# A mixture-of-experts stage: the weights of each of 32 experts are loaded once into a ring of eight, and TensorE finds a tile's weights by a register

## The chip, the cores and the metric

The kernel runs on one core of one Trainium2 chip. The metric is the device time of one execution in microseconds (us); lower is better. The core has a matrix engine (TensorE, called PE in the profile, with PEld for its weight loads), three engines that work on vectors (VectorE or DVE, ScalarE or ACT, GpSimd or POOL) and SyncE (SP), which here issues the transfers from device memory (HBM) into the on-chip memory. Each engine runs its own list of instructions; the lists meet in semaphores. Names such as PEldq and SPq are the sequencers of these engines, which run register work and bare waits.

## The reference

The program is a small two-layer decoder on 4 x 256 tokens of width 256. Layer 0 has cross-attention over 1601 context rows and then a mixture of experts, layer 1 has windowed attention and a feed-forward with weights rounded to 8-bit floats. The part that matters here is the mixture of experts of layer 0:

```
scores  = sigmoid(x @ gate_w)                       # 1024 tokens x 32 experts
selected = top 6 of the experts in the allowed groups
for each expert e and its tokens xs:                # 6144 rows in all
    d = (silu(xs @ w_gate[e]) * (xs @ w_up[e])) @ w_down[e]   # 256 -> 176 -> 256
out = sum over a token's 6 rows of weight * d  +  a shared expert of twice the width
```

## The kernel before, in words

The stage is the function `experts`. It first works out, on VectorE and TensorE, how many tokens each expert has. An expert's rows are cut into tiles of 128 rows, and the tiles of all experts stand one after the other in 80 slots (`NSLOT`; slots beyond the last tile are worked on too, with an empty token). The table `expert_of` (1 x 80, int32) says which expert a slot belongs to.

The loop runs over 96 jobs. The first 16 (`SHARED`) are the halves of the shared expert for the eight blocks of 128 tokens; their weights lie on chip. Jobs 16 to 95 are the 80 slots. For slot i the work is:

- POOL gathers the tile's rows (`gather`, L1445), eleven slots ahead, and scatters its results (`scatter`, L1450).
- PE turns the rows (`turn_rows`, L1494), multiplies them with gate and up weights (`gate_up`, L1506), turns the hidden tile (`turn_hidden`, L1513) and multiplies it with the down weights (`down`, L1523 and L1524).
- ACT applies silu (L1548) and copies the turned rows and the results (L1553, L1558).
- DVE multiplies silu with up (`hidden`, L1630) and copies the turned hidden tile out to `moe_hT` (`hidden_turned`, L1635).

All orders are written out by hand. In step j PE does `gate_up(j)`, `turn_rows` for two jobs later, `down(j - 2)` and `turn_hidden(j - 1)`. So in PE's list the down projection of one job is followed by the turn of the next job and the up projection of the one after that. In step j DVE does `hidden(j)`, `hidden_turned(j - 1)` and, in every second step from job 28 to job 90 (32 times), one part of `quantize` (L1662 to L1672): ten dependent instructions that round the weights of the last layer.

The weights lie in a ring of eight places, `wa` (gate, up and most of down, 480 KB) and `wb` (the rest of down, 48 KB). SP fills one place for each slot (`fetch`): it reads the slot's expert number into a register, and issues two transfers from the address that it gives. Slot i uses place i % 8, so PE's addresses are constants. A place is filled anew when the slot eight before has finished (`y_done`). PE waits, ahead of `gate_up`, for the count of the place's own semaphore (`load`), and ahead of `down` for the copy of the hidden tile (`ht_sb`) and for the release of its output (`added`, `y_sb`). Most waits stand on an instruction; where there are several, the others become bare wait instructions (EVENT_SEMAPHORE) on the sequencer, which the profile puts on L92 (the helper `wait`) or L1502.

Of the kernel before, what the change touches and what calls it, by code (L numbers as in the profile page):

```python
# [7 lines left out]
I32 = mybir.dt.int32  # L8
U32 = mybir.dt.uint32
F16 = mybir.dt.float16  # L10
ALU = mybir.AluOpType
# [4 lines left out]
P = 128  # L16
B, S, D = 4, 256, 256
# [3 lines left out]
DC = D // P  # L21
# [1133 lines left out]
E_ALL, TOPK, GRP, TOP_GRP = 32, 6, 4, 2  # L1155
M = 176
EXPERTS = E_ALL + 2
GU = 2 * M
REST = M - P
WA = DC * GU + D  # L1160
NSLOT = 80
# [5 lines left out]
SHARED = 2 * TT  # L1167
JOBS = SHARED + NSLOT
WRING, XRING, YRING = 8, 12, 4
CONST = {}  # L1170
for _name, _width in (("tri", P), ("before", E_ALL), ("upto", E_ALL), ("lane", P), ("slot", NSLOT), ("tokm", TT), ("spare", NSLOT), ("turn", TOPK), ("zero", D)):
    CONST[_name] = slice(sum(c.stop - c.start for c in CONST.values()), sum(c.stop - c.start for c in CONST.values()) + _width)
NCONST = CONST["zero"].stop
NCAST = CONST["upto"].stop
SPAN = 512
# [177 lines left out]
def experts(nc, t, x, wabs, wvo, wq):  # L1353

    with Scope(nc, "moe") as sc:
# [13 lines left out]
        tiles_of = sc.sb("tiles_of", [E_ALL, P], BF16)  # L1369
        raw = sc.sb("raw", [E_ALL, P])  # L1370
        last_tile, begun = sc.sb("last_tile", [E_ALL, 1]), sc.sb("begun", [E_ALL, NSLOT], BF16)
        expert_of = sc.sb("expert_of", [1, NSLOT], I32)
        base = sc.sb("base", [P, E_ALL])
        v = sc.sb("v", [P, TT, E_ALL])
        first8 = sc.sb("first8", [P, TT, 8])
# [9 lines left out]
        shared_a, shared_b = sc.sb("shared_a", [P, 2, WA]), sc.sb("shared_b", [REST, 2, D])  # L1385
        names = ["w8_in", "const_in", "shared_in", "ident_in", "zero_out", "ones_set", "pad_set", "cast_done",
                 "rank_done", "count_done", "tiles_ready", "base_done", "begun_ready", "expert_done", "expert_ready", "index",
                 "hot", "table_part", "table_ready", "rows_ready",
                 "xt_done", "xt_sb", "up_done", "silu_done", "h_done", "ht_done", "ht_sb", "y_done", "y_sb", "added", "quant", "share_step"]
        s = {n: sc.sem(n) for n in names}  # L1390
        load, stored, gathered, back = ([sc.sem(f"{n}{i}") for i in range(r)] for n, r in (("load", WRING), ("stored", YRING), ("gathered", XRING), ("back", 2)))

# [2 lines left out]
            (shared_a[:, e, :], t["wa_l"][E_ALL + e], s["shared_in"]) for e in range(2)] + [  # L1395
            (shared_b[:, e, :], t["wb_l"][E_ALL + e], s["shared_in"]) for e in range(2)] + [(w8[:, :], t["f8_l"], s["w8_in"])])
        wa, wb = sc.sb("wa", [P, WRING, WA]), sc.sb("wb", [REST, WRING, D])
        xg = sc.sb("xg", [P, XRING, D])
        xT = sc.sb("xT", [P, 3, DC, P])
        silu, h = sc.sb("silu", [P, 2, M]), sc.sb("h", [P, 2, 2 * P])  # L1400
# [3 lines left out]
        up_ps = [sc.ps(f"up{i}", [P, 512]) for i in range(2)]  # L1404
# [3 lines left out]
        count_ps, base_ps, last_ps = xt_ps[1][0:E_ALL, 0:P], xt_ps[1][:, P:P + E_ALL], xt_ps[1][0:E_ALL, P + E_ALL:P + 2 * E_ALL]  # L1408
        expert_ps, token_ps = xt_ps[1][0:E_ALL, 192:192 + NSLOT], xt_ps[1][:, 272:272 + 2 * NSLOT]

        with nc.Block() as block:
            @block.sync
            def _(sp):
                sp.wait_ge(s["const_in"], 16)
                sp.dma_start(t["xrow_s"][EMPTY:EMPTY + 1, :], const[0:1, CONST["zero"]]).then_inc(s["zero_out"], 16)
                sp.wait_ge(s["expert_ready"], 1)

                def fetch(i, u):
                    e = sp.value_load(expert_of[0:1, i:i + 1] if isinstance(i, int) else expert_of[0:1, bass.ds(i, 1)], min_val=0, max_val=E_ALL - 1)
                    sp.dma_start(wa[:, u, :], t["wa_l"][bass.ds(e, 1)].rearrange("e p n -> p (e n)")).then_inc(load[u], 16)  # L1420
                    sp.dma_start(wb[:, u, :], t["wb_l"][bass.ds(e, 1)].rearrange("e p n -> p (e n)")).then_inc(load[u], 16)

                for u in range(WRING):
                    fetch(u, u)
                with sp.Fori(1, NSLOT // WRING) as r:
                    for u in range(WRING):
                        sp.wait_ge(s["y_done"], r * WRING + (SHARED + u - WRING + 1))
                        fetch(r * WRING + u, u)
                for u in range(YRING):
                    sp.wait_ge(stored[u], 16 * (NSLOT // YRING))  # L1430
                for n in range(TT):
                    wait(sp, s["added"], SHARED + TOPK * (n - 1) if n > 1 else 0)
                    rows = t["y_s"][0:UNUSED, :].rearrange("(k t) d -> t k d", k=TOPK)
                    sp.dma_start(y6[:, n % 2, :, :], rows[n * P:(n + 1) * P]).then_inc(back[n % 2], 16)
# [27 lines left out]
            def _(pe):  # L1462
                def rank_and_count():
# [5 lines left out]
                    for n in range(TT):  # L1469
                        for m in range(n):  # L1470
                            nc.tensor.matmul(rank_ps[:, n, :], ones[:, :], selb[:, m, :], start=m == 0, stop=False)
                        last = nc.tensor.matmul(rank_ps[:, n, :], cast[:, CONST["tri"]], selb[:, n, :], start=n == 0, stop=True)
                    last.then_inc(s["rank_done"], 1)
# [16 lines left out]
                def turn_rows(i):  # L1490
# [3 lines left out]
                        last = nc.tensor.transpose(xt_ps[i % 2][:, c * P:(c + 1) * P], xg[:, i % XRING, c * P:(c + 1) * P], ident[:, :])  # L1494
                    last.then_inc(s["xt_done"], 1)

                def gate_up(j):
                    i = j - SHARED
                    wait(pe, s["h_done"], j - 1)
                    if i >= 0:  # L1500
                        pe.wait_ge(s["xt_sb"], i + 1)
                        pe.wait_ge(load[i % WRING], 32 * (i // WRING + 1))  # L1502
                    for c in range(DC):
                        rows = xT[:, i % 3, c, :] if i >= 0 else h32[:, c, j // 2 * P:(j // 2 + 1) * P]
                        w = wa[:, i % WRING, :] if i >= 0 else shared_a[:, j % 2, :]
                        last = nc.tensor.matmul(up_ps[j % 2][:, 0:GU], rows, w[:, c * GU:(c + 1) * GU], start=c == 0, stop=c == DC - 1)  # L1506
                    last.then_inc(s["up_done"], 1)

                def turn_hidden(j):
# [6 lines left out]
                def down(j):  # L1516
                    i = j - SHARED
                    pe.wait_ge(s["ht_sb"], j + 1)
                    wait(pe, s["added"], min(j - 1, SHARED))
                    wait(pe, s["y_sb"], i - 1)  # L1520
                    wd = wa[:, i % WRING, DC * GU:WA] if i >= 0 else shared_a[:, j % 2, DC * GU:WA]
                    we = wb[:, i % WRING, :] if i >= 0 else shared_b[:, j % 2, :]
                    nc.tensor.matmul(y_ps[j % 2][:, 0:D], hT[:, j % 3, 0, :], wd, start=True, stop=False)  # L1523
                    nc.tensor.matmul(y_ps[j % 2][:, 0:D], hT[0:REST, j % 3, 1, :], we, start=False, stop=True).then_inc(s["y_done"], 1)  # L1524

# [43 lines left out]
            def _(dve):  # L1569
                V = nc.vector  # L1570
                steps = [0]

                def link(ins):
                    steps[0] += 1
                    ins.then_inc(s["index"], 1)
                    dve.wait_ge(s["index"], steps[0])
# [4 lines left out]
                def tiles_and_slots():  # L1581
                    dve.wait_ge(s["const_in"], 16)
                    V.tensor_copy(cast[:, :], const[:, 0:NCAST]).then_inc(s["cast_done"], 1)
                    dve.wait_ge(s["count_done"], 1)
                    link(V.tensor_scalar(raw[:, :], count_ps, 1.0 / P, DOWN_HALF, ALU.mult, ALU.add))
                    V.tensor_scalar(tiles_of[:, :], raw[:, :], ROUND, -ROUND, ALU.add, ALU.add).then_inc(s["tiles_ready"], 1)
                    dve.wait_ge(s["base_done"], 1)
                    link(V.tensor_scalar(base[:, :], base_ps, -1.0, FAR, ALU.mult, ALU.add))
                    link(V.tensor_copy(last_tile[:, :], last_ps[:, 0:1]))
                    V.tensor_scalar(begun[:, :], const[0:E_ALL, CONST["slot"]], last_tile[:, 0:1], None, ALU.is_ge).then_inc(s["begun_ready"], 1)  # L1590
                    dve.wait_ge(s["rank_done"], 1)
                    link(V.scalar_tensor_tensor(v[:, :, :], rank_ps, -1.0, wide(base[:, :].unsqueeze(1)), ALU.mult, ALU.add))
                    link(V.tensor_tensor(v[:, :, :], v[:, :, :], sel[:, :, :], ALU.mult))
                    for n in range(TT):
                        last = V.max(first8[:, n, :], v[:, n, :])
                    link(last)
                    link(V.tensor_scalar(slot[:, :, :], first8[:, :, 0:TOPK], -1.0, FAR, ALU.mult, ALU.add))
                    link(V.tensor_scalar(tile_no[:, :, :], slot[:, :, :], 1.0 / P, -DOWN_HALF, ALU.mult, ALU.add))
                    link(V.tensor_scalar(tile_no[:, :, :], tile_no[:, :, :], ROUND, -ROUND, ALU.add, ALU.add))
                    link(V.scalar_tensor_tensor(lane_no[:, :, :], tile_no[:, :, :], -float(P), slot[:, :, :], ALU.mult, ALU.add))  # L1600
                    dve.wait_ge(s["expert_done"], 1)
                    V.tensor_scalar(expert_of[:, :], expert_ps[0:1, :], float(E_ALL - 1), None, ALU.min).then_inc(s["expert_ready"], 1)
# [618 lines left out]
```

## Time and profile before

| what | value |
|---|---|
| device time, median of 3 runs (lowest, highest) | 1879.2 us (1877.37, 1879.74) |
| the profiled execution: its own time | 1879.65 us |
| the profiled execution: span from first to last instruction | 1877.9 us |
| PE busy over the span | 1699.2 us (90%) |
| DVE busy over the span | 1413.8 us (75%) |
| HBM read, written | 111.73 MB, 25.86 MB |
| first expert tile's up projection, last one's | from 1344.0, 1577.2 us |

The times of one execution are read from the hardware profiler. Matmuls are pipelined and their ends are modelled, so a busy PE is not PE at its peak. Times in the views are microseconds from the start of the span. An entry such as "0.26 <-DVE moe_hT L1635" says how long the engine was idle before an instruction and what released it; "issue" is idle time in which it waited for nothing that the profile shows.

### The profile page before, as it was taken

The numbers are of one execution on the slowest core, as the hardware profiler recorded it, in microseconds if no ns is written. First come the engines' busy times: TensorE is split into PE (matmuls) and PEld (weight loads), VectorE is DVE, ScalarE is ACT, GpSimd is POOL, SyncE is SP. The second block draws the span as 40 slices with busy tenths as digits, with TensorE's granted clock in tenths as the row PEclk, the third lists the DMA queues.
The fourth block names the chain that finished last, engine by engine and source line by source line (L and its number), as shares of the span: only waits on it lengthen the run. The fifth ranks groups of instructions, "written<-read, shape, count | busy, mean of one in ns | idle before, by whom it ended". The sixth has DMA issues, their size and how long they took to land. (4 is left out here: it accounts for less than half of the span.)

```text
span 1877.9 us, 41481 instructions
## 1 busy us (share of the span) xinstructions
PE 1699.2 (90%) x14533; PEld 1305.7 (70%) x14679; DVE 1413.8 (75%) x3752; ACT 1096.8 (58%) x2774; POOL 1099.4 (59%) x1718
## 2 busy tenths in 40 slices
PE   4799999999999999999999999978999997289988
PEld 3677777878787788777877887756555553139974
DVE  7898887888977878878778788757566664675646
ACT  6577777767777667767676676642133332173534
POOL 5678695686776957967768568300366663181210
PEclk8899999999999999999999999997999998596998
DMA  3210110011011000200010000445298994500100
GB/s 125 74 51 30 60 58 30 19 36 47 18 38 36 18 19 18 63 27 18 20 36 18 24 1 24 148 142 206 72 280 269 273 269 153 152 11 24 46 9 23
DMA packets 74649, 140.24 MB, mean 75 GB/s; under 512 B 10921, under 2 KB 44818, under 8 KB 74194
## 3 DMA queue, kind: packets, MB, share of 16 engines
q1 hardware_dynamic: 63634, 105.37, 18.4%
q0 software_dynamic: 9984, 30.42, 4.7%
q8 instruction: 120, 1.97, 0.4%
q10 hardware_dynamic: 832, 1.84, 0.3%
q14 instruction: 79, 0.65, 0.1%
HBM read 111.73 MB, written 25.86 MB: 73 GB/s over the span
## 5 line engine op out<-in xcount | busy, mean ns | idle before, releaser
L920 DVE TENSOR_TENSOR att_pT<-att_pT 128x512 bf16<-128x512 f32 (+1 forms) x512 | 321.0, 650 | 165.9 <-ACT att_pT L729 162.9
L565 PE MATMUL att_out<-att_V,att_pT 128*128 128x128 bf16 x5760 | 386.8, 219 | 13.9 <-DVE att_pT L920 12.1
L565 PEld LDWEIGHTS att_out<-att_V,att_pT 128*128 128x128 bf16 x5760 | 349.0, 98 | 40.7 <-DVE att_pT L920 24.3
L729 ACT ACTIVATE att_pT<-att_pT 128x512 bf16<-128x512 f32 (+1 forms) x512 | 278.0, 572 | 128.8 <-PE att_pT L551 128.8
L735 ACT ACTIVATE att_prob<-att_scores,att_negmax 128x512 f32<-128x512 f32 (+1 forms) x512 | 330.3, 655 | 17.3 <-DVE att_negmax L909 16.9
L542 PE MATMUL att_scores<-att_K,att_Q 128*128 128x512 bf16 (+1 forms) x1408 | 298.3, 359 | 7.1 <-DVE att_Q L881 0.4
L907 DVE TENSOR_REDUCE att_mx<-att_scores 128x1 f32<-128x512 f32 (+1 forms) x512 | 291.3, 630 | 0.7 <-PE att_scores L542 0.6
L551 PE MATMUL att_pT<-att_ident,att_prob 128*128 128x128 f32 x1920 | 274.2, 274 | 0.0
L542 PEld LDWEIGHTS att_scores<-att_K,att_Q 128*128 128x128 bf16 x1536 | 150.5, 98 | 143.9 <-issue 1.7
L551 PEld LDWEIGHTS att_pT<-att_ident,att_prob 128*128 128x128 f32 x1920 | 208.6, 141 | 0.8
L465 PE MATMUL att_aux<-att_wkv,att_kvT 128*128 128x256 bf16 x1350 | 167.2, 273 | 17.8 <-DVE att_aT L881 15.3
L653 POOL TENSOR_TENSOR att_scaled<-att_kvraw,att_kw 128x256 f32<-128x256 f32 (+1 forms) x123 | 89.9, 731 | 135.7 <-ACT att_kvraw L697 135.7
L465 PEld LDWEIGHTS att_aux<-att_wkv,att_kvT 128*128 128x128 bf16 x1350 | 128.0, 98 | 35.6 <-DVE att_aT L881 18.8
L655 POOL TENSOR_TENSOR att_cosd<-att_scaled,att_tab 128x256 f32<-128x256 f32 (+2 forms) x153 | 127.1, 831 | 12.0
L1450 POOL DMA_INDIRECT y_s<-moe_ysb,moe_result_row x80 | 79.3, 991 | 77.3 <-ACT moe_ysb L1558 77.3
L667 POOL TENSOR_TENSOR att_rs<-att_rs,att_nhalf 128x2 f32<-128x2 f32 (+2 forms) x153 | 122.6, 801 | 0.0
L1548 ACT ACTIVATE moe_silu<-moe_up 128x176 f32<-128x176 f32 x96 | 30.5, 318 | 142.9 <-PE moe_up L1506 142.9
L1445 POOL DMA_INDIRECT moe_xg<-xrow_s,moe_token_row x80 | 77.6, 970 | 60.3 <-DVE moe_token_row L1617 35.9
L735 ACT ACTIVATION_READ_ACCUMULATOR att_prob<-att_scores,att_negmax 128x1 f32 x512 | 109.5, 214 | 0.0
L1506 PE MATMUL moe_up<-moe_wa,moe_xT 128*128 128x352 f32 x320 | 107.9, 460 | 0.0
L697 ACT ACTIVATE att_kvraw<-att_aux 128x512 f32<-128x512 f32 x120 | 68.7, 572 | 40.4 <-PE att_aux L465 40.1
L662 POOL TENSOR_TENSOR att_rs<-att_kss,att_eps 128x2 f32<-128x2 f32 (+1 forms) x123 | 30.6, 249 | 96.9 <-DVE att_kp L891 96.9
(342 smaller groups left out, 3230.2 us busy)
## 6 DMA issues: line engine op xcount, KB each, us to landing
moe_wa<-in_wa_l SPq DMA_DIRECT2D x80, 480.0 KB
att_wq<-wq_s SPq DMA_DIRECT2D x12, 512.0 KB, 3.7
att_wo<-wo_s SPq DMA_DIRECT2D x12, 512.0 KB, 3.8
moe_y<-y_s SPq DMA_DIRECT2D x8, 768.0 KB, 4.6
att_stage<-in_ctx_l SPq DMA_DIRECT2D x9, 512.0 KB, 4.3
near_s<-att_windows POOLq DMA_DIRECT2D x8, 576.0 KB, 5.6
win_near<-near_s SPq DMA_DIRECT2D x32, 144.0 KB
moe_wb<-in_wb_l SPq DMA_DIRECT2D x80, 48.0 KB
```

The costliest lines, as they stand in the source:

```text
L465: last = nc.tensor.matmul(o, kvT[:, bp, a, c, k0:k0 + P], wkv[:, par, w, c, :], start=(c, a, w) == (0, 0, 0), stop=(c, a) == (DC - 1, 1))
L542: last = nc.tensor.matmul(scores[:, lo:lo + n], Q[:, u, a, i, :], K[:, u, w, lo:lo + n], start=(a, w) == (0, 0), stop=a == 1)
L551: last = nc.tensor.transpose(pT_ps[j % 2][:, m, :], prob[:, i % 2, k0:k0 + P], ident[:, :])
L565: last = nc.tensor.matmul(out_ps[:, i % 2, :], pT[:, i % 2, a, k, :], V[:, par, k, w, :], start=(k, a, w) == (0, 0, 0), stop=(k, a) == (KT ...
L653: eng.tensor_tensor(a, raw_[:, 0:m, :], weight[:, :].unsqueeze(1).to_broadcast([P, m, HD]), ALU.mult).then_inc(linked, 1)
L655: eng.tensor_tensor(b.rearrange("p m (e f) -> p m e f", e=2), a.rearrange("p m (e f) -> p m e f", e=2), cos.unsqueeze(2).to_broadcast([P, ...
L667: eng.tensor_tensor(scale, scale, nhalf[:, 0:m], ALU.pow).then_inc(linked, 1)
L729: nc.scalar.activation(pT[:, i % 2, 0, 4 * j:4 * j + m, :], pT_ps[j % 2][:, 0:m, :], ACT.Copy).then_inc(s["pt_hi"], 1)
L735: nc.scalar.activation(prob[:, i % 2, lo:lo + n], scores[:, lo:lo + n], ACT.Exp, bias=negmax[:, i % 4:i % 4 + 1], scale=1.0, accum_out=es[ ...
L907: nc.vector.reduce_max(mx[:, i % 2, k:k + 1], scores[:, lo:lo + n], AX.X).then_inc(s["bank_max"], 1)
L920: nc.vector.tensor_tensor(pT[:, i % 2, 1, 4 * j:4 * j + m, :], pT_ps[j % 2][:, 0:m, :], pT[:, i % 2, 0, 4 * j:4 * j + m, :], ALU.subtract) ...
L1506: last = nc.tensor.matmul(up_ps[j % 2][:, 0:GU], rows, w[:, c * GU:(c + 1) * GU], start=c == 0, stop=c == DC - 1)
```

## The change

SP no longer fills a place for each slot. It loads the 32 experts in their order, each once: expert e goes to place e % 8. From the ninth on, SP first waits until all tiles of the expert eight before are done. It learns from a new table, `begun_of` (1 x 32, int32, made by DVE), at which slot an expert begins, reads that into a register and waits for `y_done` to reach it. SP also waits for the arrival of each expert's weights, four experts behind (`BEHIND`), and counts them in a new semaphore, `have`.

PE reads the slot's expert number into a register, twice for each tile: in `gate_up`, behind the wait for the turned rows, and in `down`, behind the waits there. In `gate_up` it waits until `have` is above the expert number (a wait against a register). The addresses of the weights in all four matrix products come from the register: the place is the number's lowest three bits. The first eight loads don't wait for the table `expert_of` any more.

```diff
@@ SP
-                sp.wait_ge(s["expert_ready"], 1)
-
-                def fetch(i, u):
-                    e = sp.value_load(expert_of[0:1, i:i + 1] if isinstance(i, int) else expert_of[0:1, bass.ds(i, 1)], min_val=0, max_val=E_ALL - 1)
-                    sp.dma_start(wa[:, u, :], t["wa_l"][bass.ds(e, 1)].rearrange("e p n -> p (e n)")).then_inc(load[u], 16)
-                    sp.dma_start(wb[:, u, :], t["wb_l"][bass.ds(e, 1)].rearrange("e p n -> p (e n)")).then_inc(load[u], 16)
-
-                for u in range(WRING):
-                    fetch(u, u)
-                with sp.Fori(1, NSLOT // WRING) as r:
-                    for u in range(WRING):
-                        sp.wait_ge(s["y_done"], r * WRING + (SHARED + u - WRING + 1))
-                        fetch(r * WRING + u, u)
+                def fetch(e):
+                    u = e % WRING
+                    sp.dma_start(wa[:, u, :], t["wa_l"][e]).then_inc(load[u], 16)
+                    sp.dma_start(wb[:, u, :], t["wb_l"][e]).then_inc(load[u], 16)
+
+                def report(e):
+                    sp.wait_ge(load[e % WRING], 32 * (e // WRING + 1))
+                    sp.sem_inc(s["have"], 1)
+
+                for e in range(E_ALL):
+                    if e == WRING:
+                        sp.wait_ge(s["begun_of"], 1)
+                    if e >= WRING:
+                        begun = sp.value_load(begun_of[0:1, e - WRING + 1:e - WRING + 2], min_val=0, max_val=NSLOT)
+                        sp.wait_ge(s["y_done"], begun + SHARED)
+                    fetch(e)
+                    if e >= BEHIND:
+                        report(e - BEHIND)
+                for e in range(E_ALL - BEHIND, E_ALL):
+                    report(e)
@@ PE
+                def expert(i):
+                    return pe.value_load(expert_of[0:1, i:i + 1], min_val=0, max_val=E_ALL - 1)
+
                 def gate_up(j):
...
                         pe.wait_ge(s["xt_sb"], i + 1)
-                        pe.wait_ge(load[i % WRING], 32 * (i // WRING + 1))
+                        e = expert(i)
+                        pe.wait_ge(s["have"], e + 1)
+                        first = (e & (WRING - 1)) * WA
                     for c in range(DC):
...
-                        w = wa[:, i % WRING, :] if i >= 0 else shared_a[:, j % 2, :]
-                        last = nc.tensor.matmul(up_ps[j % 2][:, 0:GU], rows, w[:, c * GU:(c + 1) * GU], start=c == 0, stop=c == DC - 1)
+                        w = wa_flat[:, bass.ds(first + c * GU, GU)] if i >= 0 else shared_a[:, j % 2, c * GU:(c + 1) * GU]
+                        last = nc.tensor.matmul(up_ps[j % 2][:, 0:GU], rows, w, start=c == 0, stop=c == DC - 1)
...
                     wait(pe, s["y_sb"], i - 1)
-                    wd = wa[:, i % WRING, DC * GU:WA] if i >= 0 else shared_a[:, j % 2, DC * GU:WA]
-                    we = wb[:, i % WRING, :] if i >= 0 else shared_b[:, j % 2, :]
+                    if i >= 0:
+                        u = expert(i) & (WRING - 1)
+                        wd, we = wa_flat[:, bass.ds(u * WA + DC * GU, D)], wb_flat[:, bass.ds(u * D, D)]
+                    else:
+                        wd, we = shared_a[:, j % 2, DC * GU:WA], shared_b[:, j % 2, :]
@@ DVE, tiles_and_slots
                     link(V.tensor_scalar(base[:, :], base_ps, -1.0, FAR, ALU.mult, ALU.add))
+                    V.tensor_scalar(begun_of[:, :], base_ps[0:1, :], 1.0 / P, None, ALU.mult).then_inc(s["begun_of"], 1)
                     link(V.tensor_copy(last_tile[:, :], last_ps[:, 0:1]))
```

## Rows read from the trace of the kernel before

**Rows 1.** Stretches: us, busy PE PEld DVE ACT POOL (x), PE clock, DMA share, GB/s

```profile
1292.80:1344.10 51.30, 47.88 (x204) 28.44 (x204) 38.10 (x101) 5.65 (x18) 11.51 (x12) 0.90 0.37 116
1344.10:1381.00 36.90, 36.90 (x159) 22.14 (x158) 18.00 (x47) 11.88 (x37) 19.64 (x20) 1.00 0.67 200
1381.00:1571.10 190.10, 189.41 (x770) 109.47 (x769) 132.88 (x448) 63.09 (x193) 119.93 (x122) 1.00 0.89 265
```

**Rows 2.** Costliest groups of the page: busy, mean ns, idle before

```profile
L1506 PE MATMUL moe_up<-moe_wa,moe_xT 128*128 128x352 f32 x320 | 107.9, 460 | 0.0
```

**Rows 3.** DMA issues of the page: count, KB each

```profile
moe_wa<-in_wa_l SPq DMA_DIRECT2D x80, 480.0 KB
```

**Rows 4.** Waits from 1381 to 1571: us in total, times, longest

```profile
PEld moe_y L1523 <- DVE moe_hT L1635: 7.9, 32, 0.3
```

**Rows 5.** Timeline of PE over one pair of tiles: start, length

```profile
1403.25 0.70 PE L1523 MATMUL moe_y<-moe_wa,moe_hT 128*128 128x256 f32 x2
...
1404.51 0.44 PE L1513 MATMUL moe_ht<-moe_ident,moe_h 128*128 128x128 f32 x2
1404.78 1.35 PE L1506 MATMUL moe_up<-moe_wa,moe_xT 128*128 128x352 f32 x4
...
1406.19 0.60 PE L1523 MATMUL moe_y<-moe_wa,moe_hT 128*128 128x256 f32 x2
...
1409.21 0.48 PE L1523 MATMUL moe_y<-moe_wa,moe_hT 128*128 128x256 f32 x1
```

**Rows 6.** Timeline of DVE over the same pair; ten quantizing instructions, first and last

```profile
1404.98 0.42 DVE L1635 COPY moe_hT<-moe_ht 128x256 f32<-128x256 f32 x1 [1.25 <-PE moe_ht L1513]
1405.33 0.22 DVE L1662 TENSOR_SCALAR moe_magic<-moe_w 128x144 int32<-128x144 int32 x1
...
1408.10 0.35 DVE L1672 TENSOR_TENSOR rest_wq<-moe_y,moe_over 128x144 bf16<-128x144 f32 x1
...
1408.74 0.41 DVE L1635 COPY moe_hT<-moe_ht 128x256 f32<-128x256 f32 x1
```

**Rows 7.** Timeline of a tile without quantizing

```profile
1349.99 0.42 DVE L1635 COPY moe_hT<-moe_ht 128x256 f32<-128x256 f32 x1
...
1351.09 0.30 PEld L1523 LDWEIGHTS moe_y<-moe_wa,moe_hT 128*128 128x128 f32 x2
...
1351.19 0.60 PE L1523 MATMUL moe_y<-moe_wa,moe_hT 128*128 128x256 f32 x2
```

**Rows 8.** SP's instructions of L1419 and L1420: ns min/median/max, first and last start

```profile
L1419 SPq FUSED_REGOPS  x152: 43/152/187, 1297.0 to 1562.5; - x152
L1419 SPq TENSOR_LOAD <-moe_expert_of x80: 263/269/481, 1296.5 to 1562.2; - x80
L1419 SPq SEQ_ASSERT  x80: 18/18/37, 1297.2 to 1562.7; - x80
L1420 SPq FUSED_REGOPS  x80: 37/37/48, 1297.3 to 1562.7; - x80
L1420 SPq MOVE moe_wa<-in_wa_l x80: 29/29/42, 1297.4 to 1562.8; - x80
```

**Rows 9.** Timeline of SP's issues, between two of its first eight loads

```profile
1301.65 0.33 SPq L1421 DMA_DIRECT2D moe_wb<-in_wb_l  x1
1302.74 0.34 SPq L1420 DMA_DIRECT2D moe_wa<-in_wa_l  x1
```

**Rows 10.** Bare waits of L92: PE 1403.7 to 1405.4, PE 1405.41 to 1405.95, ACT 1381 to 1571

```profile
nothing on L92; most used: ['L1506', 'L1524', 'L1513']
L92 PEldq EVENT_SEMAPHORE  x3: 51/51/51, 1405.5 to 1405.8; - x3
L92 ACTq EVENT_SEMAPHORE  x192: 17/17/17, 1382.3 to 1571.0; - x192
```

**Rows 11.** The table of experts: the instruction that makes it

```profile
L1602 DVE TENSOR_SCALAR moe_expert_of<-moe_xt x1: 229/229/229, 1296.2 to 1296.2; 1x80 int32<-1x80 f32 x1
```

**Rows 12.** Timeline of PE's weight loads, second last tile

```profile
1579.86 0.30 PEld L1523 LDWEIGHTS moe_y<-moe_wa,moe_hT 128*128 128x128 f32 x2 [0.75 <-DVE moe_hT L1635]
```

**Rows 13.** Timeline of DVE, last but one part of the quantizing

```profile
1562.67 0.31 DVE L1672 TENSOR_TENSOR rest_wq<-moe_y,moe_over 128x144 bf16<-128x144 f32 x1
```

More of the change, by code:

```diff
@@ L1169 @@
 WRING, XRING, YRING = 8, 12, 4
+BEHIND = 4
 CONST = {}
@@ L1371, in experts @@
         last_tile, begun = sc.sb("last_tile", [E_ALL, 1]), sc.sb("begun", [E_ALL, NSLOT], BF16)
-        expert_of = sc.sb("expert_of", [1, NSLOT], I32)
+        expert_of, begun_of = sc.sb("expert_of", [1, NSLOT], I32), sc.sb("begun_of", [1, E_ALL], I32)
         base = sc.sb("base", [P, E_ALL])
@@ L1388, in experts @@
                  "hot", "table_part", "table_ready", "rows_ready",
-                 "xt_done", "xt_sb", "up_done", "silu_done", "h_done", "ht_done", "ht_sb", "y_done", "y_sb", "added", "quant", "share_step"]
+                 "xt_done", "xt_sb", "up_done", "silu_done", "h_done", "ht_done", "ht_sb", "y_done", "y_sb", "added", "quant", "share_step", "begun_of", "have"]
         s = {n: sc.sem(n) for n in names}
@@ L1397, in experts @@
         wa, wb = sc.sb("wa", [P, WRING, WA]), sc.sb("wb", [REST, WRING, D])
+        wa_flat, wb_flat = wa[:, :, :].rearrange("p w n -> p (w n)"), wb[:, :, :].rearrange("p w n -> p (w n)")
         xg = sc.sb("xg", [P, XRING, D])
```

## The prediction

> **What bounds the kernel now.** The change lies in one stage, the expert loop, so I read the windows view first, by stretch: sixteen jobs of the shared experts up to 1344, the first expert tiles alone up to 1381 (13 up projections, 36.9 us, 2.84 each), 64 tiles beside the quantizing of the last layer's weights up to 1571 (2.97 each) [rows 1]; a few are left. PE counts as busy nearly all the time in the two middle stretches, and the DMA share is 0.89 there. That looks like two limits, so the next question is whether PE ever waits for a weight. It does not: the first matmul that reads a fetched weight has 0.0 us of idle time before it over all 320 instructions [rows 2], although 80 loads of 480 KB (and 80 of the small part) run beside it [rows 3]. The loads are hidden now.
>
> What PE does wait for is the view of waits: in the stretch with quantizing, 32 times, for the copy of the turned hidden tile (moe_hT) by DVE, 7.9 us in all [rows 4]. The two timelines show why. A pair of tiles takes from 1403.25 to 1409.21, 5.96 us [rows 5]. DVE ends a copy of moe_hT at 1405.40, quantizes from 1405.33 to 1408.45 and ends the next copy at 1409.15; the down projection starts at 1409.21, 0.05 us later [rows 6]. From it 1.26 us pass to the next turn of the hidden tile, 1404.51 [rows 5], and about 0.9 us to the end of its copy, 1405.40. So the loop down projection, turn, copy, quantize, copy, down projection sets the pair: 1.26 + 0.9 + 3.75 + 0.05 = 5.96. The other tile of a pair has air: copy done at 1405.40, down projection at 1406.19. In tiles without quantizing PE itself is the limit: the copy is done at 1350.41, weights for the down projection are loaded at 1351.09 and it starts at 1351.19, 0.78 us later [rows 7].
>
> **Part one: 48 loads fewer.** 32 of 80 loads stay. They were hidden, so on the path this is worth 0. The cover for the 32 that stay only grows: an expert's place is refilled when its eighth successor is due, and its arrival is reported four experts later. 1024 tokens with 6 experts each are 192 per expert, two tiles; three experts lie between the one whose end lets the report run and the one that needs it, some six tiles less the two that the down projection trails, four tiles or 12 us. SP needs there one register load and two issues, under 2 us [rows 9]. SP's first eight loads no longer wait for the table of experts and start earlier; PE doesn't reach them until 1344 in either case.
>
> **Part two: a small instruction on DVE.** The integer table of first tiles stands in the chain ahead of the loop. The nearest row is the other table of this kind, 229 ns [rows 11]. Cost 0.2 us (bounds 0 and 0.3).
>
> **Part three: registers on PE.** Each of 80 tiles now loads an expert number into a register twice: ahead of the up projection, and ahead of the down projection, behind the wait for moe_hT. No PE row shows this, but SP has done it 80 times: TENSOR_LOAD 269 ns, FUSED_REGOPS 152, SEQ_ASSERT 18, and for an address FUSED_REGOPS 37 and MOVE 29 [rows 8], 0.505 us of work. With the handovers between them SP takes from the end of one issue, 1301.98, to the next, 1302.74: 0.76 us [rows 9]. On PE the nearest thing is its bare waits: 51 ns each, where ACT's take 17, and the four of a tile (three of L92, one between them) start within 1405.5 to 1405.8 [rows 10], about 0.10 to 0.13 us apart, so 0.05 to 0.08 of handover. Five handovers on top of 0.505 give 0.76 to 0.9. I take 0.86, near the PE end. The bounds are 0.505 (no handover) and 1.3 (all but the TENSOR_LOAD three times as dear, as the waits are, plus handover).
>
> Can PE's sequencer do this ahead of time? Rows 10 decide: at 1403.7 to 1405.4 no bare wait runs, and three run right after the copy ended at 1405.40, though the down projection itself started only at 1406.19 [rows 5]. The first of them belongs to the turn behind that down projection, and what it asks for is the copy before, which had released a down projection at 1403.25 [rows 5]. So the sequencer stood at the wait for moe_hT and passed nothing; when released it ran almost a tile ahead of the array. The new register load stands behind just this wait. By the Trainium skill (Perfetto Trace Analysis, Tensor Engine Instruction) an instruction of PE waits in a queue and the sequencer is free at once, and TensorE: Matmul & The Clock Gate, opening table, gives that queue 64 places; this case's rows don't agree for waits on semaphores (no wait in the 1.7 us up to 1405.4). By that rule part three would be hidden but for the load behind the copy; by the rows it isn't.
>
> So every down projection can start 0.86 us after its copy at the earliest, and the rest is air.
> - 32 late tiles beside quantizing: 0.05 us becomes 0.86, and the delay lies in the loop, so 32 x 0.81 = 25.9 us. Behind the waiting load stand the down projection, the turn and the next up projection; the turn feeds the copy ahead of the next quantizing, so nothing takes it back.
> - The last two tiles, also late (the load of weights waits for the copy at 1579.86 [rows 12]): 1.6 us.
> - 14 tiles without quantizing (twelve at the start, two near the end): weights are loaded 0.1 us ahead of the matmul, so the air is 0.68 us; 0.86 - 0.68 = 0.18, 2.5 us.
> - The other 32 tiles: 0.18 us later each, hidden by DVE's 3.1 us of quantizing. If that cover went, 5.8 us.
> - The load ahead of the up projection: after release the sequencer needs 0.86, a second address and two waits (about 0.4), a register load (0.7), the register wait with its sum (0.2) and an address (0.2), 2.4 us; the array needs 0.86 + 1.26 + 0.27 (1404.51 to 1404.78 [rows 5]) = 2.4 us to get there. Just hidden; I add 0.1 us for the 14 tiles that PE sets, 1.4 us. The late tiles have slack.
>
> Sum: 25.9 + 1.6 + 2.5 + 1.4 + 0.2 = 31.6 us on the profiled execution's 1879.65, which is 0.45 above the median shown: **1911 us**.
>
> **The rivals.**
> *PE's sequencer becomes the bound.* Per tile it would have to do two TENSOR_LOADs (0.54), other new register work of 0.72 (twice 152 + 18, four addresses of 37 + 29, three steps of 37 ns for sum and masks), a wait, 18 handovers of 0.07 (1.26) and the four old waits (0.5): 3.05 us. The tile now takes 2.84 or 2.97 [rows 1]. At single prices this is less than the longer pair allows. With the register work twice as dear it is 3.8, and 64 x 0.8 + 16 x 0.95 gives +65, 1945; three times, 4.5, gives 64 x 1.5 + 16 x 1.65, +122, 2002. It decides from about 3.4 us a tile. For it: 51 against 17 ns [rows 10]. Against: DVE's and ACT's other prices are not known to scale so. The Trainium skill (Vector Engine (DVE) Microarchitecture Reference, Instruction fetch and dispatch) says that the firmware's short way for moves and register arithmetic is built for SP's sequencer alone; it gives no price, and no row here shows PE doing either.
> *Hidden.* The sequencer gets past the wait, or the work costs well under 0.1 us: 1880. For it: the sequencer does run a tile ahead elsewhere. Against: rows 10.
> *Faster, by the memory traffic.* The pair is set by DVE's chain; if the loads' writes slow DVE, fewer loads shorten it. The last step of quantizing takes 0.35 at 1408.10 [rows 6] and 0.31 at 1562.67, when the loads have nearly ended [rows 13]; the whole quantizing is 3.12 us at 1405.33 and could win 0.1 us by what changes there. 32 x 0.1 is 3.2 us, 1876, if part three costs nothing; it decides only if a register load costs less than 0.15 us. Against: TENSOR_LOAD alone is 0.269 [rows 8].
> *The register load waits until the array is empty.* Then each of 160 costs a refill of about 1 us, +150, 2030. Against: the bare waits run beside the array.
>
> **How the numbers follow.** Main line 0.55 (0.505 gives 34 x 0.455 + 0.2 = +16, 1895; 1.3 gives 34 x 1.25 + 14 x 0.62, +51, 1931; its own range is 1895 to 1931). Sequencer as the bound 0.22, half of it under 1975. Hidden 0.11, of which 0.02 would still be over the 0.2% (3.8 us, about what a measurement of this kernel can tell from no change). Faster 0.05. Emptied array 0.07. The range takes in the main line, the hidden case and the nearer half of the bound: 1880 to 1975. Faster 0.05, same 0.09, slower 0.86.
>
> **What the profile after would show.** Right: the first weights load of the down projection starts 0.8 to 0.9 us after each copy of moe_hT ends; pairs of 6.8 us; TENSOR_LOAD on PE's queue between the copy and that load; 0.0 us before the up projection's matmuls; DMA share under 0.5 in the stretch. Sequencer as the bound: idle time put down to "issue" ahead of the up projection, too, and equal tiles with and without quantizing. Wrong: pairs of 5.96 with the register work done before the copy ends, or a down projection that starts within 0.1 us of it.

## The result, and the profile after

| | before | after |
|---|---|---|
| device time, median (lowest, highest) | 1878.35 us (1877.37, 1879.74), 4 runs | 1911.99 us (1909.61, 1913.05), 4 runs |
| ratio to before, 95% interval | | 1.0177 [1.0159, 1.0194] |
| span of the profiled execution | 1877.9 us | 1907.8 us |
| HBM read | 111.73 MB | 85.78 MB |

The change costs 33.6 us by the medians, 1.8%. The windows view of after, in the three stretches of [rows 1] (the second and the third end again at the up projection of the same tile as there), shows where:

```profile
core 0: us, PE busy (x) PEld busy (x) DVE busy (x) ACT busy (x) POOL busy (x), PEclk, DMA share, GB/s
1292.90:1344.20 51.30, 47.43 (x202) 28.38 (x202) 37.47 (x98) 5.65 (x18) 11.54 (x12) 0.92 0.33 106
1344.20:1383.60 39.40, 39.40 (x158) 22.50 (x157) 17.99 (x47) 11.81 (x37) 19.68 (x20) 1.00 0.40 133
1383.60:1599.90 216.30, 201.33 (x770) 111.32 (x769) 131.62 (x448) 63.08 (x193) 119.78 (x122) 1.00 0.40 123
```

Up to the first expert tile nothing moved: 51.3 us in both. The 13 steps without quantizing take 39.4 us instead of 36.9. The first two of them, in which PE still does down projections of the shared expert, take 2.83 us each as before; the other eleven take 3.07 instead of 2.84. The 64 tiles beside the quantizing take 216.3 us instead of 190.1, 26.2 more. The granted clock is 1.00 in both stretches, as before, so it isn't the clock. The DMA share falls from 0.89 to 0.40, and the time grows all the same.

The groups of the page that answer to [rows 2, 3]:

```profile
L1523 PE MATMUL moe_up<-moe_wa,moe_xT 128*128 x320 | 112.2, 473 | 0.1
...
moe_wa<-in_wa_l SPq DMA_DIRECT2D x32, 480.0 KB, 3.1
```

32 loads are left of 80, and PE still never waits for weights ahead of the up projection (0.1 us of idle time over 320 matmuls). What it waits for is in the waits view of after, stretch 1384 to 1600, to be held against [rows 4]:

```profile
PEld moe_y L1543 <- issue: 27.5, 59, 0.9
...
PE moe_y L1543 <- issue: 14.9, 32, 0.6
```

The idle time stands at the same place, ahead of the down projection, but the releaser is no longer DVE's copy. It is "issue": nothing that the profile shows as a wait, and the rows of PE's sequencer below show what stands in that time. The first line is the one to compare with [rows 4]: weight loads waited 32 times before, 7.9 us in all, and now 59 times, 27.5 us. The timelines of a pair of tiles, first PE's, then DVE's (start, length):

```profile
1429.48 0.69 PE L1543 MATMUL moe_y<-moe_wa,moe_hT 128*128 x2 [0.48 <-issue]
1430.11 0.70 PE L1544 MATMUL moe_y<-moe_wb,moe_hT 48*128 x2
1430.74 0.44 PE L1530 MATMUL moe_ht<-moe_ident,moe_h 128*128 128x128 f32 x2
...
1432.53 0.69 PE L1543 MATMUL moe_y<-moe_wa,moe_hT 128*128 x2
...
1436.22 0.69 PE L1543 MATMUL moe_y<-moe_wa,moe_hT 128*128 x2 [0.46 <-issue]
```

```profile
1428.17 0.41 DVE L1656 COPY moe_hT<-moe_ht 128x256 f32<-128x256 f32 x1
...
1431.21 0.42 DVE L1656 COPY moe_hT<-moe_ht 128x256 f32<-128x256 f32 x1 [1.69 <-PE moe_ht L1530]
1431.55 0.22 DVE L1683 TENSOR_SCALAR moe_magic<-moe_w 128x144 int32<-128x144 int32 x1
...
1434.92 0.41 DVE L1656 COPY moe_hT<-moe_ht 128x256 f32<-128x256 f32 x1
```

The copy ends at 1435.33, and the down projection that needs it starts at 1436.22: 0.89 us, where it was 0.05 in [rows 5, 6]. The pair takes 6.74 us (1429.48 to 1436.22) instead of 5.96. What fills the 0.89 us is on PE's sequencer. The rows of lines L1510 (the register load) and L1543 (the down projection's first product), minimum, median and maximum in ns, over the whole program, and then the register load between 1428.5 and 1429.3:

```profile
L1510 PEldq TENSOR_LOAD <-moe_expert_of x160: 295/302/610, 1342.3 to 1613.6; - x160
L1510 PEldq FUSED_REGOPS  x160: 151/151/165, 1342.9 to 1613.9; - x160
L1510 PEldq SEQ_ASSERT  x160: 18/18/24, 1343.1 to 1614.1; - x160
...
L1543 PEldq ALU_OP  x80: 32/32/32, 1351.2 to 1614.2; - x80
L1543 PEldq FUSED_REGOPS  x80: 60/60/60, 1351.3 to 1614.3; - x80
...
L1510 PEldq TENSOR_LOAD <-moe_expert_of x1: 309/309/309, 1428.6 to 1428.6; - x1
```

The copy before the down projection of 1429.48 ended at 1428.58, and the load starts at 1428.6. The sequencer did stand at the wait and did none of the register work ahead of time; over all 80 tiles of this trace the load starts 0.04 us after the end of its copy. Its five instructions are 302 + 151 + 18 + 32 + 60 = 563 ns; the other 0.33 us are the steps between them.

The same 0.89 us explain the tiles without quantizing. From a down projection to the next turn are 1.26 us (1429.48 to 1430.74), from there to the end of its copy 0.89 (1431.63), and then the register work: 1.26 + 0.89 + 0.89 = 3.04 us for one round of down projection, turn, copy, registers. That is more than the 2.84 us that PE needs for a tile, so by this sum the loop sets them all, where before (1.26 + 0.89 + 0.05 = 2.20) it had air. The experiments try it.

### The profile page after: what moved, and what is told of

It is laid out like the page before. It is cut to its first block and busy times, and to the rows that moved or that the text cites. A ratio compares the mean times of both kernels' runs of the same rounds, so it can differ in the third digit from the quotient of the medians.

```text
span 1907.8 us, 41828 instructions
## 1 busy us (share of the span) xinstructions
PE 1713.7 (90%) x14533; PEld 1306.3 (68%) x14679; DVE 1412.3 (74%) x3753; ACT 1096.9 (57%) x2774; POOL 1099.9 (58%) x1718
## 3 DMA queue, kind: packets, MB, share of 16 engines
HBM read 85.78 MB, written 25.86 MB: 59 GB/s over the span
## 5 line engine op out<-in xcount | busy, mean ns | idle before, releaser
L1523 PE MATMUL moe_up<-moe_wa,moe_xT 128*128 x320 | 112.2, 473 | 0.1
L1656 DVE COPY moe_hT<-moe_ht 128x256 f32<-128x256 f32 x96 | 40.4, 420 | 73.1 <-PE moe_ht L1530 73.1
```

Source lines behind the costliest of these rows:

```text
L1523: last = nc.tensor.matmul(up_ps[j % 2][:, 0:GU], rows, w, start=c == 0, stop=c == DC - 1)
```

## The experiments

The theory: register work that stands between the copy's release and the down projection lies in the loop between PE and DVE. X is the time from the end of the copy to the down projection; a tile then takes the greater of 2.84 (PE) and X + 2.15, and a pair with quantizing at least X + 2.15 + 3.70 (1431.63 to 1435.33, from copy to copy). The rivals: PE's sequencer is too slow for a tile's instructions wherever they stand, and the loads' traffic counts for something. The kernel before was run again beside the experiments, with medians from 1877.6 to 1879.5 us; ratios are to the kernel before of the same round, and differences of a microsecond or two between rounds say nothing.

**Moving the load.** The register load of the down projection is put ahead of its wait:

```diff
 def down(j):
+    if i >= 0:
+        u = pe.snap(expert(i) & (WRING - 1))
     pe.wait_ge(s["ht_sb"], j + 1)
...
-        u = expert(i) & (WRING - 1)
```

> The changed kernel, but in the down projection the expert number is loaded ahead of the wait for moe_hT instead of behind it; the number and kind of instructions stay. Theory (what costs time is the register work that stands between the release by the copy and the down projection): the two loading steps leave that place and one register step of 32 ns, one address step of 60 ns and their handovers stay, so the down projection of a late tile starts about 0.25 us after its copy instead of 0.89; 34 x 0.2 us over the kernel before, 1886 us (1881 to 1892). Rival A (PE's sequencer is short of time in total, wherever the work stands): the total is the same, so 1912. Rival B (the new loads, or the waits for them, cost the time): 1912, as nothing of them changes.

1885.4 us (1882.66 to 1886.49, 10 runs), 1.0027 [1.0017, 1.0037] of before. Same 160 loads, same instructions, 26.6 us less than after. A late tile in it: DVE's copy, PE's down projections at both ends of the pair, what is left behind the wait, and the up projections over the loop:

```profile
1430.43 0.42 DVE L1657 COPY moe_hT<-moe_ht 128x256 f32<-128x256 f32 x1
...
1424.94 0.69 PE L1544 MATMUL moe_y<-moe_wa,moe_hT 128*128 x2 [0.22 <-DVE moe_hT L1657]
...
1431.12 0.69 PE L1544 MATMUL moe_y<-moe_wa,moe_hT 128*128 x2 [0.25 <-DVE moe_hT L1657]
...
L1544 PEldq ALU_OP  x80: 32/32/32, 1352.9 to 1590.7; - x80
L1544 PEldq FUSED_REGOPS  x80: 60/60/60, 1353.0 to 1591.0; - x80
...
L1523 PE MATMUL moe_up<-moe_wa,moe_xT x320: 459/459/558, 1346.6 to 1586.0; 128*128 x160
```

X is 0.27 here (1430.85 to 1431.12): the address for the down weights, 32 + 60 ns and the steps around it, is still worked out behind the wait. By the theory a pair takes 0.27 + 5.85 = 6.12; it takes 6.18. The releaser is DVE's copy again. The loop from the first to the last tile's up projection takes 239.4 us, 6.0 more than before's 233.4 (1344.1 to 1577.5), and 32 x 0.22 of X would be 7.0. Of the change's cost, the place of one register load is thus all but some 6 us. The 13 steps without quantizing answer the first rival:

```profile
1346.60:1383.40 36.80, 36.80 (x159) 22.03 (x157) 17.95 (x47) 11.85 (x37) 19.63 (x20) 1.00 0.43 137
```

They are back at 36.8 us, 2.83 each, with both register loads in every tile. So PE's sequencer gets through a tile with two loads in 2.83 us or less, and its total is not what makes 3.07 of it in after.

**One load for a tile, its place kept.** The number is loaded at the up projection, and the ring place stays in a register for the down projection:

```diff
+place = {}
 def gate_up(j):
-    e = expert(i)
+    e = pe.snap(expert(i))
+    place[i] = pe.snap(e & (WRING - 1))
     pe.wait_ge(s["have"], e + 1)
-    first = (e & (WRING - 1)) * WA
+    first = place[i] * WA
...
 def down(j):
-    u = expert(i) & (WRING - 1)
+    u = place[i]
```

> The changed kernel, but the expert number is loaded once for each tile, ahead of the up projection, and the place in the ring is kept in a register until the down projection two jobs later. Behind the wait for moe_hT only one address step of 60 ns is left. Theory: late tiles start about 0.17 us after their copy, 34 x 0.12 us over the kernel before, 1883 us (1879 to 1888). Rival A (total time of the sequencer): a third of the new register work is gone, so about two thirds of the 33 us stay, 1895 to 1903. Rival B (loads): 1912.

1880.47 us (1878.4 to 1883.07, 10 runs), 1.0003 [0.9993, 1.0012]: no difference to before that can be measured. A late tile's copy and down projection, the one register instruction that stands ahead of the latter, and the up projections:

```profile
1429.61 0.41 DVE L1659 COPY moe_hT<-moe_ht 128x256 f32<-128x256 f32 x1
...
1430.16 0.69 PE L1546 MATMUL moe_y<-moe_wa,moe_hT 128*128 x2
...
L1546 PEldq FUSED_REGOPS  x80: 46/46/46, 1353.0 to 1586.8; - x80
...
L1526 PE MATMUL moe_up<-moe_wa,moe_xT x320: 459/459/558, 1346.7 to 1582.1; 128*128 x160
```

X is 0.14 us, and the loop 235.4 us, 2.0 over before; 32 x 0.09 = 2.9 would be the theory's.

**The registers without the loads' part.** The kernel before, its 80 loads untouched, with the register loads and addresses of the change alone (the slot's own place is kept, by adding a shifted number that is always zero; that is a shift and an addition more, in the trace one register instruction more ahead of the down projection):

```diff
 # gate_up
+    e = expert(i)
+    first = (((e >> 5) + i % WRING) & (WRING - 1)) * WA
...
 # down, behind its waits
-    wd = wa[:, i % WRING, DC * GU:WA] if i >= 0 else shared_a[:, j % 2, DC * GU:WA]
+    u = ((expert(i) >> 5) + i % WRING) & (WRING - 1)
+    wd, we = wa_flat[:, bass.ds(u * WA + DC * GU, D)], wb_flat[:, bass.ds(u * D, D)]
```

> The kernel before, with its 80 loads, its ring by slot and its waits for them, and with the register part of the change alone: the expert number is loaded twice for each tile at the same two places, and the addresses come from a register that always holds the slot's own place (the number shifted right by five, which is 0, plus a constant). One register step more stands ahead of each address than in the changed kernel. Theory: the whole cost is there, and about 0.1 us more for each late tile: 1915 us (1908 to 1922). Rival B (the new loads and the waits for them cost the time): 1879 to 1885. Rival A expects 1912 or more, too.

1919.26 us (1917.97 to 1922.0, 4 runs), 1.021 [1.019, 1.0231]. So the registers bring all of the cost by themselves, 40 us over before in the same round (1879.5), and the extra instruction can account for what is over 33.6 (X is 0.12 us longer than in after; 34 late tiles and 14 without quantizing, 48 x 0.12 = 5.8):

```profile
1431.30 0.41 DVE L1644 COPY moe_hT<-moe_ht 128x256 f32<-128x256 f32 x1
...
1425.87 0.69 PE L1532 MATMUL moe_y<-moe_wa,moe_hT 128*128 x2 [0.41 <-issue]
...
1432.72 0.69 PE L1532 MATMUL moe_y<-moe_wa,moe_hT 128*128 x2 [0.35 <-issue]
```

X is 1.01 and the pair 6.85 (theory: 1.01 + 5.85 = 6.86).

**A second load behind the wait.** The address of the small part of the down weights comes from a load of its own:

```diff
-        wd, we = wa_flat[:, bass.ds(u * WA + DC * GU, D)], wb_flat[:, bass.ds(u * D, D)]
+        again = expert(i) & (WRING - 1)
+        wd, we = wa_flat[:, bass.ds(u * WA + DC * GU, D)], wb_flat[:, bass.ds(again * D, D)]
```

> The changed kernel with a second load of the same expert number behind the wait for moe_hT (it serves the second address). One more load is 0.30 + 0.15 + 0.02 us and three handovers of 0.08, 0.7 us. Theory: it lies in the path in the 34 late tiles and in the 14 tiles without quantizing, 48 x 0.7, so 1912 + 33 = 1945 us (1938 to 1955). Rival A (total): all 80 tiles pay, 1912 + 56 = 1968. Its partner, the same load ahead of the up projection, follows; by the theory that one costs under a third of this.

1944.77 us (1944.08 to 1945.31, 4 runs), 1.0341 [1.0323, 1.036]. Copy and down projections of one pair, and the waits from 1384 to 1575:

```profile
1430.78 0.42 DVE L1657 COPY moe_hT<-moe_ht 128x256 f32<-128x256 f32 x1 [2.00 <-PE moe_ht L1530]
...
1429.06 0.69 PE L1544 MATMUL moe_y<-moe_wa,moe_hT 128*128 x2 [0.78 <-issue]
...
1432.74 0.69 PE L1544 MATMUL moe_y<-moe_wa,moe_hT 128*128 x2 [0.36 <-issue]
...
PE moe_y L1544 <- issue: 29.1, 52, 0.8
```

X is 1.54, and a tile takes 3.68 us (1429.06 to 1432.74); the theory's 1.54 + 2.15 is 3.69. Idle time stands ahead of the down projection alone.

**A second load ahead of the up projection.** The same extra load, on the other side:

```diff
     e = expert(i)
+    again = expert(i)
     pe.wait_ge(s["have"], e + 1)
-    first = (e & (WRING - 1)) * WA
+    first = (again & (WRING - 1)) * WA
```

> The changed kernel with a second load of the same expert number ahead of the up projection (it serves the addresses), 0.7 us more of the sequencer's time for each tile, the same amount as in the run with two loads behind the wait for moe_hT. Theory: beside quantizing the pair is set by the copy, the register work ahead of the down projection and the quantizing; the later up projection has about 0.7 us of air in a pair, so only the 14 tiles without quantizing pay, 14 x 0.7, and at most 0.05 in the rest: 1922 us (1915 to 1928). Rival A (total): as much as its partner at the least, 1945, or 80 x 0.7, 1968.

1916.46 us (1913.48 to 1917.76, 4 runs), 1.0195 [1.0177, 1.0214]: 4.5 us over after for 80 loads, where the same 80 behind the copy brought 32.8. This is under the 1922 expected. PE's timeline and the waits, 1384 to 1575:

```profile
1425.70 0.60 PE L1544 MATMUL moe_y<-moe_wa,moe_hT 128*128 x2
...
1427.51 1.45 PE L1524 MATMUL moe_up<-moe_wa,moe_xT 128*128 x4 [0.21 <-issue]
...
1429.01 0.60 PE L1544 MATMUL moe_y<-moe_wa,moe_hT 128*128 x2
...
PE moe_up L1524 <- issue: 16.4, 51, 0.8
```

The idle time has changed its place: it stands ahead of the up projection, and none ahead of the down projection. This is what the first rival looks like: with three register loads PE's sequencer sets the tile, 3.31 us for this one (1425.70 to 1429.01) and 3.40 on average (269.2 us from the first up projection, 1346.3, to the last, 1615.5, less 1.0 for the last tile's own, over 79 steps). With two loads it is not the limit, as the load put ahead of its wait showed, but one more load makes it so. The expectation counted a whole load, 0.7 us, for each tile without quantizing; such a tile went from 3.07 only to this bound, which fits a time at the low end of its range.

**Rounding left out, in both kernels.**

```diff
 def quantize(n):
-    w, done = w8[:, part], QUANT_STEPS * n
...
-    then(V.tensor_tensor(wq_flat[:, part], y8[:, :], over[:, :], ALU.subtract), QUANT_STEPS)
+    V.tensor_copy(wq_flat[:, part], w8[:, part])
```

In the kernel after:

> The changed kernel with the ten quantizing instructions of each part replaced by one copy (the rounding of the last layer's weights is left out). Theory: no copy of moe_hT is late any more, and every tile costs what one without quantizing costs in the changed kernel, 3.07 us; a pair goes from 6.76 to 6.14, 31 x 0.62 = 19 us less: 1893 us (1888 to 1898). With the partner below the change is then worth about 23 us instead of 33, because a tile without quantizing hides most of the register work. Rival A (total): the sequencer sets the tiles, with quantizing or without, so little is won here, 1905 to 1912.

In the kernel before:

> The kernel before with the same ten instructions replaced by one copy (rounding left out). Every tile costs 2.84 us, a pair 5.67 instead of 5.96, 32 x 0.29 = 9 us less: 1870 us (1867 to 1873). Rival A expects the same here, and so a difference to the changed kernel's partner of 33 us or more; theory expects about 23.

1889.62 us (1889.36 to 1894.06, 4 runs), 1.0066 [1.0045, 1.0086], and 1868.79 us (1865.9 to 1869.7, 4 runs), 0.9944 [0.9925, 0.9963]. The up projections over the loop, of the kernel after without rounding and of the kernel before without it:

```profile
L1523 PE MATMUL moe_up<-moe_wa,moe_xT x320: 459/459/558, 1344.9 to 1588.0; 128*128 x160
```

```profile
L1506 PE MATMUL moe_up<-moe_wa,moe_xT x320: 459/459/462, 1344.2 to 1568.7; 128*128 128x352 f32 x160
```

243.1 against 224.5 us, 18.6 more, and 20.8 us by the medians. This is the second case of the theory by itself: less 1.0 and 0.9 us for the last tile's own products, over 79 steps, a tile of after takes 3.06 us without quantizing, by the sum above 3.04, for PE's 2.83. The rest of the cost, about 13 us, needs the quantizing between the copies.

**Rounding in halves.** Five of the ten instructions in every step from job 28, so that no copy comes late, first in the kernel before, then with the kept place of the second experiment (`half` 0 holds the steps 1 to 5, the other half 6 to 10):

```diff
-def quantize(n):
+def quantize(n, half):
...
+    if half == 0:
...
+    else:
...
...
-if j >= SHARED + 12 and j % 2 == 0 and part < PARTS:
+if j >= SHARED + 12 and part < PARTS:
...
-    quantize(part)
-    part += 1
+    quantize(part, j % 2)
+    part += j % 2
```

> The kernel before with each part of the rounding halved: five of its instructions in every step from job 28 instead of ten in every second step. If the loop down projection, turn, copy, rounding, copy sets the pair of late tiles, no tile is late any more: a copy is followed by about 1.6 us of rounding instead of 3.1, which fits into a tile of 2.84 us that PE sets. 64 tiles then cost 2.84 instead of 2.97 each: 0.13 x 64 = 8 us less, 1870 (1867 to 1874). If instead the memory traffic of the 80 loads slows the stretch, halving the rounding changes nothing: 1878.

> The changed kernel with one register load for each tile, at the up projection, whose place is kept for the down projection, and with the rounding halved as in the run beside it. If register work counts only behind a copy that is waited for, it counts nowhere here: 1870 (1867 to 1875), within 0.2% of the split kernel of before, since 48 loads fewer are worth nothing where no load is waited for. If fewer loads free memory traffic that DVE and PE feel, it is faster than that one by over 0.2%, under 1866. If PE's sequencer is near its limit, slower, 1885 and more.

1871.51 us (1868.76 to 1872.03, 5 runs), 0.9961 [0.9948, 0.9974], and 1870.09 us (1867.67 to 1871.2, 6 runs), 0.9953 [0.9941, 0.9966]. Both are faster than both kernels, by 0.4 to 0.5% of before, with intervals that end below 1. Between them lie 1.4 us, and their runs overlap. Their up projections, the split kernel of before first:

```profile
L1506 PE MATMUL moe_up<-moe_wa,moe_xT x320: 459/459/462, 1344.5 to 1569.0; 128*128 128x352 f32 x160
```

```profile
L1526 PE MATMUL moe_up<-moe_wa,moe_xT x320: 459/459/462, 1344.1 to 1568.6; 128*128 x160
```

224.5 us in both. With 80 loads or 32, with constants or with one register load for a tile, the loop runs at PE's pace: 48 loads fewer are worth nothing here that can be measured. That says nothing yet of DVE's chain, which sets no tile in these two.

## Why the prediction was right

1911 was predicted, 1911.99 measured, and the runs support the way there: the register load stands behind the wait for the copy, and its time lies in the loop between PE and DVE. That the total comes within 1 us is partly luck. It was added to a run 1.3 us above the median of before, so the 31.6 us predicted stand against 33.6 measured, and terms that were off in both directions made up for each other.

- *The sequencer stands at the wait.* Shown: the load starts within 0.1 us of the copy's end (1428.58, 1428.6), and put ahead of the wait it gives back 26.6 of 33.6 us. The rule of the Trainium skill that was weighed (Perfetto Trace Analysis, Tensor Engine Instruction: a matmul or weight load is pushed into a wait queue, and the sequencer is ready for the next instruction) isn't tried by after, where the wait stands on the register load itself. In the kernel before it stands on a weight load, and there the trace doesn't agree: in all 64 tiles beside the quantizing no bare wait ran in the 1.7 us up to the end of the copy, and the next one ran 0.06 us behind it.
- *X.* 0.86 predicted, 0.89 measured, and by different parts: TENSOR_LOAD 302 ns where SP's 269 was taken, FUSED_REGOPS and SEQ_ASSERT the same 151 and 18, and for the address an ALU_OP of 32 and a FUSED_REGOPS of 60 instead of 37 + 29. The work is 0.563 instead of 0.505, and five steps of about 0.065 us lie in the range of 0.05 to 0.08 that was read from the bare waits. That 0.86 came so near is in part luck, as it was a choice within 0.76 to 0.9.
- *Late tiles.* 25.9 predicted, and 0.28 for one tile without quantizing whose down projection falls into this stretch, 26.2; measured 26.2 (216.3 - 190.1 for the stretch of 64). Two small errors cancel here: the delay of a late tile is 0.84 us and not 0.81 (32 x 0.03 = 1.0), and the quantizing became a little shorter, by 1.2 us (last step, 11.0 us in all before and 9.8 in after, shown under the rivals).
- *Tiles without quantizing.* Eleven of the 14 have their down projection in the first stretch and were to cost 0.28 each with the share of the up projection, 3.1; measured 2.5, or 0.23 each. The reason given was the missing air ahead of the down projection; the fuller one is the loop of 3.04 us, which the prediction didn't add up for these tiles. It gives 0.20 a tile.
- *The load ahead of the up projection.* "Just hidden" holds: 0.1 us of idle time over 320 matmuls. Its 1.4 us can't be told apart from the line before.
- *The small instruction on DVE.* Its 0.2 us can't be seen: the first expert tile's up projection starts at 1344.2 us for 1344.1, and between 1344.1 and 1346.8 in the other runs.
- *The end of the loop* was mis-sized. To the last down projection the two kernels stand like this, before first:

```profile
L1523 PE MATMUL moe_y<-moe_wa,moe_hT x160: 379/379/483, 1351.2 to 1582.4; 128*128 128x256 f32 x160
```

```profile
L1543 PE MATMUL moe_y<-moe_wa,moe_hT x160: 379/406/787, 1351.5 to 1615.0; 128*128 x160
```

From the end of the third stretch to there are 15.1 us instead of 11.3: 3.8 where 2.2 had been counted (1.6, and 0.28 for each of two tiles). Most of the difference is the granted clock in the last tile, which the prediction left out. Just ahead of the last down projection it is like this, before first:

```profile
1581.00:1582.60 1.60, 1.08 (x5) 0.50 (x4) 0.43 (x1) 0.39 (x1) 0.72 (x1) 1.00 0.20 82
...
1612.00:1613.50 1.50, 1.06 (x4) 0.29 (x2) 0.41 (x1) 0.38 (x1) 0.36 (x1) 0.50 0.00 0
```

It was still 1.00 before and is 0.50 in after, the lower of its two levels, 1.2 GHz; PE had been idle for 1.35 us ahead of the down projection at 1610.64. From there to the last one, at 1614.41, are 3.77 us where the loop gives 3.04, and the last one's own first product took 0.3 us longer: 1.0 of the 1.6 us. Another 0.3 is that the two tiles ahead of the late ones have no rows left to turn, so that PE needs 2.62 and 2.61 us for them before and lost 0.43 each to the loop.

In sum the loop is 2.5 + 26.2 + 3.8 = 32.5 us longer, for 31.6 predicted, and 33.6 by the medians. The span grew by 29.9 only, since what follows the last down projection took 292.8 us instead of 295.5. That doesn't follow the change: the kernel of before with the registers has 295.8 (1917.0 - 1621.2), and the split kernel of before 292.9 (1867.0 - 1574.1):

```profile
L1523 PE MATMUL moe_y<-moe_wa,moe_hT x160: 379/379/653, 1351.6 to 1574.1; 128*128 128x256 f32 x160
```

- *The rivals.* The sequencer as the bound: not in after. Its price of 3.05 us a tile (the terms add up to 3.07) was too high, as the same 160 loads pass at 2.83 when one stands ahead of the wait; but one more load ahead of the up projection reaches the bound at 3.3 to 3.4 us, where it was to decide. Hidden: excluded by the change's own time. A load that waits for an empty array: excluded by 160 loads at 1885.4 us; no run shows such a refill, and the prediction took its 1 us from no row. Faster by the memory traffic: PE isn't slowed by the loads, as the two split kernels show (224.5 us each). DVE's last step of quantizing did get shorter, as that rival read it. These are its lines before, in after, with the load ahead of its wait, and with the registers in the kernel before (busy time, mean in ns):

```profile
L1672 DVE TENSOR_TENSOR rest_wq<-moe_y,moe_over 128x144 bf16<-128x144 f32 x32 | 11.0, 345 | 1.1
...
L1693 DVE TENSOR_TENSOR rest_wq<-moe_y,moe_over 128x144 bf16<-128x144 f32 x32 | 9.8, 308 | 1.1
...
L1694 DVE TENSOR_TENSOR rest_wq<-moe_y,moe_over 128x144 bf16<-128x144 f32 x32 | 10.9, 340 | 1.1
...
L1681 DVE TENSOR_TENSOR rest_wq<-moe_y,moe_over 128x144 bf16<-128x144 f32 x32 | 9.8, 307 | 1.1
```

It doesn't follow the loads: 32 loads go with 308 and with 340 ns, 80 loads with 345 and with 307. So their number doesn't set it; what does wasn't tried. It is worth 1.2 us at the most.

## What to carry to other kernels

In these runs a wait in PE's list held back the bare waits and the register work that stood behind it. What doesn't depend on the wait (a register load, a mask, an address) belongs ahead of it, at best where PE has work to cover it. Before taking away transfers, look whether anything waits for them: here 48 of 80 loads went for nothing, and the price was paid in the narrowest place of the loop. And when a loop over two engines sets the time, spreading the second engine's side work over all rounds can win what fewer transfers didn't: 0.4% here.

## What the runs showed of the hardware

- The steps of a register load cost PE about what they cost SP (FUSED_REGOPS 151 and 152 ns, SEQ_ASSERT 18 and 18, the TENSOR_LOAD itself 302 and 269). The address of a product costs PE one FUSED_REGOPS of 46 or 60 ns, where SP has 37 and a MOVE of 29. The factor of three between PE's and ACT's bare waits, from which the sequencer's rival was priced, isn't found in them.
- A register load isn't always 302 ns. In after the 80 behind the copy took 316 ns at the most, the 80 ahead of the up projection 297 to 610, half of them more than 470. The one behind the first down projection of the pair above:

```profile
L1510 PEldq TENSOR_LOAD <-moe_expert_of x1: 485/485/485, 1429.9 to 1429.9; - x1
```

It ran while that down projection's matmuls did. That alone isn't the reason: with two loads behind the wait, the load at the same place has a median of 304 ns beside the same matmuls, and the one at 1428.6 (309 ns) ran beside the end of an up projection. What lengthens it wasn't tried, and stays open.
